# First loads of a perceiver kernel in another order, with matmuls over zeros ahead of the first product

## The reference, cut to what matters

```python
x = x + _L0_xattn_ref(_layernorm(x), ctx_2048, mask, Wq, Wk, Wv, Wqf, Wkf, ...)   # linear attention with ReLU features
x = x + _L0_attn_ref(...);  x = x + _L0_ffn_ref(...)
x = x + _L1_xattn_ref(_layernorm(x), ctx_2048, Wq, Wkv, ...)                       # keys and values quantised
...
x = x + _L3_ffn_ref(...)
```

## Time and profile before

| | |
|---|---|
| Median of 3 runs | 1051.53 us (1050.83 to 1052.58) |
| The profiled execution, its own time | 1052.45 us |
| Its span in the trace | 1050.6 us |
| PE busy | 991.0 us, 94% of the span |
| DVE busy | 715.7 us, 68% |
| ACT busy, POOL busy | 358.4 us, 157.4 us |
| Bytes moved | 76.21 MB |

### The profile page before, as it was taken

One profiled execution on the slowest core, in us unless ns is written; L12 is line 12 of the kernel. 1 busy time (PEld: TensorE's weight loads), 2 busy tenths in 40 slices (PEclk: granted clock), 3 DMA queues, 4 the chain that ended last, 5 costly groups with the idle time before them and its releaser, 6 DMA issues.

```text
span 1050.6 us, 20593 instructions
## 1 busy us (share of the span) xinstructions
PE 991.0 (94%) x7812; PEld 655.7 (62%) x7836; DVE 715.7 (68%) x1910; ACT 358.4 (34%) x627; POOL 157.4 (15%) x144
## 2 busy tenths in 40 slices
PE   6999999998889988998999999999999999988898
PEld 4776766665335544466777777676777777743455
DVE  3776767768788935887676767667676767843444
ACT  2333332334328721542333333333333332311211
POOL 0000000000100010242222223222322223000000
PEclk9999999999999999998999999999999999899999
DMA  7100100102239996960000000000000000232440
GB/s 287 41 22 21 40 20 22 38 5 83 82 88 196 189 309 242 348 211 2 1 1 1 2 0 0 0 0 0 0 0 0 0 1 2 80 141 86 164 175 3
DMA packets 69000, 76.21 MB, mean 73 GB/s; under 512 B 52560, under 2 KB 59728, under 8 KB 65104
## 3 DMA queue, kind: packets, MB, share of 16 engines
q1 hardware_dynamic: 68512, 74.84, 23.5%
q10 hardware_dynamic: 432, 0.62, 0.2%
HBM read 62.54 MB, written 0.07 MB: 60 GB/s over the span
## 4 chain that ended last, share of the span: by engine, by line
PE 73%; DVE 11%; issue 6%; ACT 3%; POOL 3%; DMA 3%; SPq 0%; DVEq 0%; POOLq 0%
PE ps L2232 15%; PE ps L2126 12%; PE ps L1483 8%; PE ps L2222 7%; PE ps L1473 4%; PE ps L1494 4%; PE ps L1517 2%; PE ps L1529 2%; POOL x_sum L2751 2%; ACT vals L2031 2%; DVE S L2437 1%; PE ps L513 1%; DMA x_keys<-vals 1%; PE ps L1883 1%; PE ps L2835 1%
## 5 line engine op out<-in xcount | busy, mean ns | idle before, releaser
L2232 PE MATMUL ps<-vals,S 128*128 128x257 f32 x784 | 188.6, 384 | 0.7 <-ACT S L2683 0.7
L2126 PE MATMUL ps<-keysT,row_biases_sb 128*128 128x512 f32 (+1 forms) x416 | 186.4, 574 | 0.1
L2751 POOL TENSOR_TENSOR x_sum<-x_max,consts 128x4 f32<-128x4 f32 (+1 forms) x104 | 133.4, 1282 | 321.7 <-DVE x_max L2425 321.7
L2437 DVE SCALAR_TENSOR_TENSOR S<-ps,x_sum,keysT 128x128 f32<-128x128 f32 x392 | 110.9, 344 | 73.0 <-PE ps L2232 64.2
L2232 PEld LDWEIGHTS ps<-vals,S 128*128 128x128 f32 x784 | 143.4, 192 | 19.0 <-issue 1.0
L2683 ACT ACTIVATE S<-S 128x512 f32<-128x512 f32 (+1 forms) x104 | 62.7, 606 | 219.1 <-DVE S L2472 218.5
L2222 PE MATMUL ps<-x_q,x_keys 128*128 128x128 f32 x784 | 113.9, 287 | 0.0
L2126 PEld LDWEIGHTS ps<-keysT,row_biases_sb 128*128 128x128 f32 x416 | 76.7, 192 | 56.3 <-issue 51.2
L2222 PEld LDWEIGHTS ps<-x_q,x_keys 128*128 128x128 f32 x784 | 96.1, 192 | 0.1
L1483 PE MATMUL ps<-ring,S 128*128 128x512 f32 x196 | 92.2, 593 | 0.9 <-DVE ps L1624 0.9
L2615 ACT COPY x_keys<-ps 128x512 f32<-128x512 f32 (+1 forms) x104 | 57.1, 549 | 66.3 <-PE ps L2126 33.5
(11 more groups left out here) (455 smaller groups left out, 1364.9 us busy)
## 6 DMA issues: line engine op xcount, KB each, us to landing
ring<-weights SPq DMA_DIRECT2D x24, 1024.0 KB, 6.7
keysT<-ctxT SPq DMA_DIRECT2D x2, 3136.0 KB, 14.9
vals<-ctxN SPq DMA_DIRECT2D x1, 6272.0 KB, 26.9
S<-ctxT SPq DMA_DIRECT2D x12, 512.0 KB, 4.0
ring<-weights SPq DMA_DIRECT2D x6, 768.0 KB, 7.3
keysT<-weights SPq DMA_DIRECT2D x1, 1792.0 KB, 8.8
keysT<-weights SPq DMA_DIRECT2D x1, 1536.0 KB, 12.0
row_biases_sb<-row_biases SPq DMA_DIRECT2D x1, 1416.0 KB, 12.8
```

The costliest lines, as they stand in the source:

```text
L2126: ins = pe.matmul(ps[:, x2_key_bank(g, c), 0:width(c)], x2_wk[:, k, :], ctxT[:, k, span(c)], start=k == 0, stop=k == KT - 1)
L2232: ins = pe.matmul(bank(6, D + 1), S[:, a:a + TILE], ctx_and_ones[:, SUB * c + s, :], start=c == 0 and s == 0, stop=c == NC - 1 and s == su ...
L2437: ins = dve.scalar_tensor_tensor(S[:, a:a + TILE], ps[:, 3 + c % 2, 128 * s:128 * s + 128], x2_inv[:, c % 2, s:s + 1], x2_tile_const, ALU. ...
L2751: pool.tensor_tensor(x2_inv[:, c % 2, 0:n], x2_var[:, c % 2, 0:n], C("neg_half").broadcast_to([128, n]), ALU.pow)\
```

## The change

Seven edits:

- `sweep_first_half` loads chunk 0 in two transfers of 256 tokens (256 KB each); the first signals `ctx_first`, the second `ctx_in0`. SP issues the first where the whole chunk was issued, and the second behind the rest of `pre` and ahead of `x`. All later issues of SP come one transfer later.
- The first `keys_T` waits for `ctx_first`; the second one, of the other half, waits for `ctx_in0`.
- PE begins with a wait for `sw_zeros` and 18 matmuls of 128 x 512 (bf16) over the cleared `sw_value_absmax`, into bank 7, which nobody reads.
- The wait for `pre_features` moves from behind the first `keys_T` to ahead of the first `features`.
- The wait for the constants moves to ahead of the second pair's step.
- The wait for `sw_sums_zeros` stays where it was.
- ACT loads its table of functions first, then waits for the key weights, then issues the constants.

```diff
+        def sweep_first_half(sp, half):
+            tokens = slice(TWO * half, TWO * half + TWO)
+            sp.dma_start(sw_ctxT[0][:, :, tokens], io["ctxT"][:, :, tokens]).then_inc(sem("ctx_first" if half == 0 else "ctx_in0"), 16)
...
-                if half == 0:
+                if isinstance(pair, int) and pair == 0:
+                    pe.wait_ge(sem("ctx_first"), 16)
+                elif half == 0 or (isinstance(pair, int) and pair == 1):
                     pe.wait_ge(sem(f"ctx_in{ph}"), loaded * 16)
...
                 if n == 2:
                     value_and_key(pair, ph, half, 1)
+                if first:
+                    weights_here(pe, "pre_features")
                 features(pair, n)
...
+            pe.wait_ge(sem("sw_zeros"), 1)
+            none = sw_value_absmax.bitcast(BF16)
+            for _ in range(18):
+                pe.matmul(bank(7), none[:, 0:128], none, start=True, stop=True)
             pe.wait_ge(sem("key_weights_in"), 16)
             keys_T(0, 0, 0, 2, 1)
             weights_here(pe, "pre")
-            weights_here(pe, "pre_features")
-            pe.wait_ge(sem("constants_in"), 16)
             pe.wait_ge(sem("sw_sums_zeros"), 2)
 
             def four_pairs(i, first=False):
                 for q in range(4):
+                    if first and q == 1:
+                        pe.wait_ge(sem("constants_in"), 16)
                     pair_step(i * 4 + q, q % 2, q // 2, q % 2, 2, first=first and q == 0)
...
                 sp.dma_start(W("pre")[:, 0:n_keys], io["weights"][:, a:a + n_keys]).then_inc(sem("key_weights_in"), 16)
-                SWEEP_LOADS[0](sp, 0)
+                SWEEP_LOADS[2](sp, 0)
                 sp.dma_start(W("pre")[:, n_keys:], io["weights"][:, a + n_keys:a + pieces[0][2]]).then_inc(sem("weights_in0"), 16)
+                SWEEP_LOADS[2](sp, 1)
             sp.dma_start(x[:, :], io["x"]).then_inc(sem("x_in"), 16)
...
                 act.dma_start(mask_sb[:, :], io["mask"]).then_inc(sem("mask_in"), 16)
+            act.preload_act_table_set("exp_and_others")
+            if sweep:
+                act.wait_ge(sem("key_weights_in"), 16)
             act.dma_start(consts[:, :], io["constants"]).then_inc(sem("constants_in"), 16)
-
-            act.preload_act_table_set("exp_and_others")
             act.wait_ge(sem("columns_in"), 16)
```

More of the change, by code:

```diff
@@ L1728, in perceiver @@
         SWEEP = (sweep_tensor, sweep_vector, sweep_scalar, sweep_pool)
-        SWEEP_LOADS = (sweep_first_load, sweep_loads)
+        SWEEP_LOADS = (sweep_first_load, sweep_loads, sweep_first_half)
         x0_qT = cut(scratch(0, KT * T), KT, T)
```

## The result

The changed kernel is slower: 1055.05 us in the median of 17 runs (1050.15 to 1058.14) against 1052.04 us (1048.90 to 1053.69) for the kernel before in as many; the ratio is 1.0030 with a 95% interval of 1.0017 to 1.0043, so 3.0 us with 1.8 to 4.5. A second measurement further down gave 1.0026 (1.0007 to 1.0045). The forecast was 1053.2 us from a median of 1051.53, +1.7 us. The sign came as forecast, the size is larger; 1055.05 lies 1.85 us above the likeliest value and just inside the upper end of the range, 1055.3.

A forecast was written before the change was run, and what follows sets the result against it. PE, busy 94% of the span, bounds the kernel, at the start once `kv1` and DVE's memset release it. 1052.45 + 0 (first product, `kv1` wait, constants, other waits) + 1.7 (clock) = 1054.15, 1053.2 on the median; range 1050.4 to 1055.3.

The forecast's parts named there:

- What decides at the start: PE's start: the memset behind `kv1` holds the first L1483 until 12.88 us; an earlier first `keys_T` is worth 0.
- Clock behind the gate, +1.7: First L1483 product after PE's wait for the memset: longer idle time drops the clock for 3.4 us, costing 1.7 us.
- Rival A: Clock after PE's wait for the memset stays down 6.8 us; +2.5 to +3.4 us, 1054.0 to 1054.9; chance 0.17.
- the gain of 1.35 us: First `keys_T` at full clock behind the 18 matmuls: saves 1.35 us, counted as 0 because PE then waits anyway.
- the product behind the gate, which ran at the full clock before: Premise of the 1.7 us clock loss: L1483's four matmuls from 12.88 took 1.95 us against 1.72 later.
- The gate, 0: PE's wait for DVE's memset behind `kv1`: same 2,112 KB on SP's queue, `kv1` lands at 12.3 as before; 0 us.
- the end of +0.6: Slower bound for `kv1`'s landing: SP's one additional issue costs 0.6 us if the queue ever ran empty.
- The end of -1.5: Faster bound for `kv1`'s landing: 1.5 us earlier if the constants fell wholly behind it.
- From the start to the end: Sweep: a microsecond PE wins or loses after 12.88 us is one in the end time, until the last tiles.
- Constants, other waits: Start: constants land at about 11.4 us, 2.1 us of slack before POOL's `rstd`; moved waits not last either; 0 us.
- D: Start: constants land later than about 14.5 us and DVE's first tile holds PE; landing at 15.5 costs 1 us; chance 0.04.
- C: Start: constants yield to SP's queue, `kv1` and memset up to 1.5 us earlier; 1050.0, or 1051.7 with clock loss; chance 0.09.

The follow-up runs named there:

- e3: Changed kernel plus 14 more matmuls over zeros between the first `keys_T` and the wait for DVE's memset; ratio 1.0006 to the kernel before.
- e1: Changed kernel without the 18 matmuls over zeros; ratio 1.0012 to the kernel before.
- e2: Kernel before with only the 18 matmuls over zeros added ahead of the first `keys_T`; ratio 0.9998 to the kernel before.
- e4: Changed kernel with DVE's memset moved ahead of its waits for `x` and `kv1`; ratio 1.0009 to the kernel before.
- e5: Changed kernel with ACT's order undone, constants issued first and function table behind them; ratio 1.0007 to the kernel before.
- e0: Kernel before, run again without any edit; ratio 1.0004 to the kernel before.
- e6: Kernel before with only DVE's memset moved ahead of its waits for `x` and `kv1`; ratio 0.9969 to the kernel before, 0.9988 when repeated.
- e7: Changed kernel with DVE's memset early, `kv1` issued right behind the rest of `pre`, layer norm behind the first four pairs; ratio 0.9963 to the kernel before, 0.9964 repeated.
- e9: Kernel before, third profile, without any edit; ratio 1.0001 to the kernel before.

## Why the prediction was right, and where it was off

**What decides at the start.** Right in every profile that kept the gate. `kv1` ends the wait, PE's releaser is the memset, and the first product gains nothing by being early: it was through at 9.7 us in place of 11.9, and the gate opened at 13.57 in place of 12.88.

**Clock behind the gate, +1.7.** Right in mechanism, and in size against a good profile of the kernel before: 8.13 us from the gate to the second `keys_T` against 6.43, 1.70 us, with a slow stretch of 3.4 us wholly on dense work. e3 shows the cause, e1 that the fillers aren't it. Rival A, the long slow stretch, happened in neither profile of the changed kernel, but in e1 (9.41 us, 3.0 lost), e2, e4 and e5 (8.84 us, 2.4 lost), and e5 differs from the changed kernel only in ACT's order. Which length comes hung on where the fall came: in the changed kernel's two profiles behind the gate (idle times of 3.83 and 3.40 us), in e1 and e5 inside the wait (4.87 and 4.38 us). So at the start the reason for taking 3.4 us and not 6.8, that dense work is followed by the short stretch, held: PE was busy for all of 3.40 us in the short ones and for 1.5 to 2.8 us of the first 3.4 in the long ones. At 297.1 it did not: that stretch lasted 6.8 us with the same 3.04 of 3.40 us busy in its first half as the short one of the earlier trace rows. The idle time was forecast at 4.2 us and measured 3.83 and 3.40. The rule of the Trainium skill (TensorE: Matmul & The Clock Gate, "Part 1: The HAM clock gate") that activity releases the throttled clock agrees with the first `keys_T`, 1.89 us right behind the fillers against 3.34 to 3.75 without; the gain of 1.35 us that it would have given is, as the sum had it, ahead of the gate.

**The term that was off: "the product behind the gate, which ran at the full clock before".** It rested on one profile. In e0 the kernel before also passed the gate slowly, with the clock not yet up. Over its three profiles the way from gate to second `keys_T` is 7.08 us, against 8.13 for the changed kernel, so the term is worth 1.05 us on the average and 1.7 against a good execution.

**The gate, 0.** Mis-sized. `kv1` was taken to land at 12.3; the gate stood at 12.88, 12.30 and 12.25 in the kernel before and at 13.57 and 13.02 in the changed one, 0.82 us later by the means. That is within the end of +0.6 plus the spread. The end of -1.5, for constants that yield to SP's queue, has nothing for it: with the constants held back `kv1` landed at 12.35 to 12.96, without (e5) at 12.40. With the term above it makes 1.86 us at the second `keys_T` (19.56 against 21.42 by the means) and 1.83 at the reduction (249.75 against 251.58). That the forecast of +1.7 is nearly this is luck: it was 1.7 for the clock and 0 for the gate, where the means of two profiles and three say 1.05 and 0.8.

**From the start to the end.** The text said that a microsecond lost by PE in the sweep is one in the end time. The sweep bears it out, 1.86 and 1.83. The measured end times say 3.0 (1.8 to 4.5) and 2.7 (0.7 to 4.7): 1.83 lies inside both intervals, near the lower edge of the first. The 1 us between stays open. The lower mean clock of the changed kernel's executions points to the slow stretches of later stages, whose part varies by 7 us among the fourteen profiles, and which the forecast put at nothing. The other kernels warn against reading the end time off one profile's sweep. Against the mean of the kernel before the reduction comes 3.2 us later in e1 and 2.4 in e2, and their times differ by 1.3 us (-0.4 to 2.9) and -0.2 us (-1.7 to 1.3); in e6 it comes 0.3 us earlier and the time is 3.3 us lower (1.5 to 4.9). A microsecond at the sweep was not one in the end time there, or these profiles aren't typical of their executions. And the measured 1055.05 is in the range only because its upper end was drawn for rival A, which did not come.

**Constants, other waits, D and C.** The constants landed at 3.77 + 8.5 = 12.3, 0.9 us later than the 11.4 forecast, and 1.9 us ahead of POOL's `rstd` at 14.24, which DVE released. No cost. The rival of a faster side, C, needed `kv1` well before 12.3, and no profile with the changed order of loads and the gate kept has it (12.40 to 12.96).

## What to carry to other kernels

Before loads are reordered, find which of several waits at one place comes last, and follow it back to its transfer: here chunk 0 was the longest wait in the list and worth nothing, the `kv1` rows the one that counted. Work that is made early ahead of a wait that stays turns into idle time of the matrix engine, and that costs the clock on the work behind. With the gate opened, `kv1` issued earlier and the layer norm moved out of the way besides, the kernel is 0.37% faster than the one before (e7). And where the clock moves freely, read the effect of an early edit at the end of its stage in several profiles, and the mean clock over all executions beside it: the kernel before scattered by 2.0 us at the end of the sweep (three profiles) and by 4.8 us at the end (17 runs).

## What the runs showed of the hardware

The same program can start with or without the clock: between e0 and e9, identical kernels, L1483 took 3.75 and 1.96 us behind idle times of 1.08 and 1.48 us. Every idle time of 2.9 us and more at the start was followed by a slow stretch: it began inside the idle time (at 14.7, within the 3.01 us of e4) or up to 1.4 us behind its end (at 13.75 behind the 3.83 us of the changed kernel, at 10.8 behind the 2.89 us of e2, which ended at 9.46). It lasted 3.4 us twice and 6.8 us four times. The landing time of one and the same transfer, behind the same bytes, scattered by 1.2 us (11.64 to 12.88), which is as much as most edits at a start are meant to bring.
